# Graph attention and routed experts: slots between the third and fourth score step, three row scatters a turn for the next graph

## The chip, the core and the metric

The kernel runs on one core of a Trainium2 chip. The metric is the time of one execution in device microseconds (us); lower is better. A core has TensorE (PE: matrix products and transposes), VectorE (DVE), ScalarE (ACT), GpSimd (POOL) and SyncE (SP). Each has its own list of instructions and runs it in order; they wait for each other by semaphores.

## The reference

Sixteen graphs of 512 nodes with 128 features. With x normalised over its features (feat):

```python
h = feat @ W
logits = swap(h @ a_1) + h @ a_2 + (h @ a_12) @ swap(h)
e = where(adj > 0, leaky_relu(logits, 0.2), NEG_INF)
h_prime = softmax(e) @ feat
x = x + elu(feat @ W_1 + h_prime @ W_2)
```

Here a graph's attention runs over its own 512 nodes. Then the tokens, x normalised again, go through 16 experts of which the two with the highest gate logits count:

```python
topk_vals, topk_idx = top_k(xn @ gate_w + gate_b, 2)
moe = sum_k softmax(topk_vals)_k * (relu(xn @ w1[e_k] + b1[e_k]) @ w2[e_k] + b2[e_k])
x = x + layernorm(xn + moe) * gamma + beta
```

## The kernel before

The kernel has a **graph stage** and an **expert stage**. The graph stage ends with each token's normalised row written twice (once for each of its two experts) into a table in device memory, `expert_bins`, sorted by expert. The expert stage loads tiles of 128 rows of that table, runs the two products of their expert, and scatters the results.

A graph has 4 tiles (`TPG`) of 128 nodes. The graph stage is a software pipeline: `turns(body)` (line 258) runs `body(k)` on each engine with k from -2 to 18 (19 on GpSimd), and in a turn k each engine works on several graphs at once. `has(k, n)` says whether graph k - n exists. In turn k, in the order of the engines' lists:

- Graph k: scores (PE L733 and L734, DVE L923), with relu (ACT L563) and exponential (ACT L567). PE adds the mask `no_edge` to the product of queries and features; DVE joins it with the relu and finds the row minimum. There are four score steps a turn, one for each tile.
- Graph k - 1: transposes of the probabilities (PE L724), their copies (ACT L558 for tiles 0 to 2, DVE L931 for tile 3) and the products with the values (PE L742). ACT's copy of tile 2 waits for TensorE's product of tile 0 as well.
- Graph k - 2: ELU (DVE L937, L940, L948, L952; ACT L572), statistics of the rows (DVE L907, L912), one over the root of the variance on GpSimd (`rstds`, L475 and L480), normalised rows (DVE L969).
- Graph k - 3: row transposes (PE L773), gate logits (PE L781), the top two experts (DVE `gate`, L1043 to L1064), `ranks` (PE L752 and L754: how many tokens before this one go to the same expert), `slot` (DVE L1071 to L1089: the row number of each token in the table, from the ranks and a running count `base`). `slot` also needs `gate_exp` (ACT L615).
- Graph k - 4: eight row scatters (GpSimd L485, `scatter_row`), each an indirect DMA of 128 rows of 520 bytes, one for each tile and each of the two experts.
- Graph k + 1: feature transposes (PE L789, copied by ACT L590), queries, and at the turn's end the edge mask `no_edge` (DVE L901), made of the int32 adjacency of 128x2048 elements. The next turn's first score step waits for it.

**GpSimd's turn.** Its list in a turn is written by hand. Eight places for scatters stand between waits for steps of VectorE and ScalarE of graph k (`after_masked`: score step n done, `after_prob`: n exponentials done) and the two `rstds`. In a turn k before the change all eight places take rows of graph k - 4, whose slots were made in the turn before. The waits only place the scatters in time; the data do not need them.

**VectorE's turn** has, at its end: score steps 2 and 3, copy of tile 3, `slot(k - 3)`, `feature_shift`, `mask(k + 1)`, `rows(k - 2)`. **TensorE's** has scores 2, feature transposes of graph k + 1, ranks of graph k - 3, scores 3, values 1, queries, values 2 and 3. **ScalarE's** has, from the middle: exps 1, relu 2, features copy, rows_out, gate_exps, relu 3, exps 3, queries copy, exps 2, features.

**From stage to stage.** When the last `slot` is done, VectorE makes the table of tiles (L1112 to L1164), which TensorE helps to spread over the partitions (L838). SyncE and ScalarE write padding rows (L390, L659: eight DMAs each). SyncE waits for the table, the padding and all row scatters before it loads the first tile (L419).

Of the kernel before, what the change touches and what calls it, by code (L numbers as in the profile page):

```python
# [20 lines left out]
def graph_attention_and_routed_experts(nc, x, adj, W, a_1, a_2, a_12, W_1, W_2, gate_w, gate_b, w1, b1, w2, b2,  # L21
# [7 lines left out]
    K = 2  # L29
# [25 lines left out]
    with ExitStack() as ctx:  # L55
# [164 lines left out]
        def settle(eng):  # L220

            eng.sem_inc(s_settled[eng.engine.name], 1)
# [40 lines left out]
        def has(k, back):  # L263

            return not isinstance(k, int) or 0 <= k - back < G
# [178 lines left out]
        def _(pool):  # L444
# [47 lines left out]
            def after_prob(k, n):  # L492
                if has(k, 0):
                    pool.wait_ge(s_exp, k * TPG + n)

            def body(k, b, h):
                if has(k, 4):
                    pool.wait_ge(s_slot, k - 3)
                    pool.wait_ge(s_row_out, k - 3)
                    settle(pool)  # L500
                    scatter_row(k - 4, 0, 0)
                    after_masked(k, 0)
                    scatter_row(k - 4, 0, 1)
                    after_prob(k, 1)
                    scatter_row(k - 4, 1, 0)
                    after_masked(k, 1)
                    scatter_row(k - 4, 1, 1)
                if has(k, -2):
                    rstds(0, k + 3, s_mv1, s_rs1)
                if has(k, 4):  # L510
                    scatter_row(k - 4, 2, 0)
                if has(k, 2):
                    rstds(TPG, k - 1, s_mv2, s_rs2)
                if has(k, 4):
                    after_masked(k, 2)
                    scatter_row(k - 4, 2, 1)
                    after_masked(k, 3)
                    scatter_row(k - 4, 3, 0)
                    after_prob(k, 3)
                    scatter_row(k - 4, 3, 1)  # L520
            turns(body, 4)


# [176 lines left out]
        def _(pe):  # L700
# [96 lines left out]
            def body(k, b, h):  # L797
                if has(k, 1):
                    prob_transposes(k - 1, 0)
                if has(k, 0):  # L800
                    scores(k, b, 0)
                if has(k, 1):
                    prob_transposes(k - 1, 1)
                if has(k, 0):
                    scores(k, b, 1)
                if has(k, 3):
                    rows_transposes(k - 3)
                if has(k, 0):
                    features_products(k, b)
                if has(k, 3):  # L810
                    logits(k - 3)
                if has(k, 1):
                    prob_transposes(k - 1, 2)
                    prob_transposes(k - 1, 3)
                    values(k - 1, 1 - b, 0)
                if has(k, 0):
                    scores(k, b, 2)
                if has(k, -1):
                    features_transposes(k + 1)
                if has(k, 3):  # L820
                    ranks(k - 3)
                if has(k, 0):
                    scores(k, b, 3)
                if has(k, 1):
                    values(k - 1, 1 - b, 1)
                if has(k, -1):
                    queries(k + 1, 1 - b)
                if has(k, 1):
                    values(k - 1, 1 - b, 2)
                    values(k - 1, 1 - b, 3)  # L830
            turns(body)


# [57 lines left out]
        def _(dve):  # L891
# [106 lines left out]
            def body(k, b, h):  # L998
# [24 lines left out]
                    stats(k - 2, TPG, s_bn2, s_mv2)  # L1023
                if has(k, 0):
                    scores(k, 2)
                    scores(k, 3)
                if has(k, 1):
                    pt_copy(k - 1, 3)
                if has(k, 3):
                    slot(k - 3)  # L1030
                if has(k, -2):
                    feature_shift(k + 2)
                if has(k, -1):
# [248 lines left out]
```

## Time and profile before

| what | us |
|---|---|
| median of 3 runs | 612.57 |
| lowest and highest | 611.96, 614.91 |
| the profiled execution's own time | 614.96 |
| its span, first to last instruction | 613.2 |
| mean granted TensorE clock | 0.905 |

The graph stage takes the first 306 us, the hand-over to the expert stage up to about 330 us, the expert stage the rest. In the rows, a timeline line has the start, the busy time, the engine, the line of the kernel, the operation and what it writes and reads. In square brackets stands how long the engine was idle before it and what ended that. PEld are weight loads of TensorE. A granted clock of 1.00 is 2.4 GHz, 0.50 is 1.2 GHz.

### The profile page before, as it was taken

What the parts mean: (1) busy time and instruction counts of PE and PEld (TensorE: products, weight loads), DVE (VectorE), ACT (ScalarE), POOL (GpSimd) and SP (SyncE); (2) the same over time, 40 slices, a digit from 0 to 9 for tenths busy, and PEclk for the clock granted to TensorE, in tenths of its full rate; (3) what the DMA queues carried; (4) which work ended last, traced back from release to release, by engine and by line L of the source; (5) the groups of instructions that cost most, each with busy time, mean ns of one, the idle gap of its engine ahead of it and who ended that gap; (6) DMA issues with size and microseconds to landing.
All of it is one profiled execution on the core that took longest, in us unless ns stands there. A gap on an engine that the chain in (4) does not pass through costs nothing.

```text
span 613.2 us, 12119 instructions
## 1 busy us (share of the span) xinstructions
PE 464.1 (76%) x2950; PEld 372.8 (61%) x2972; DVE 388.1 (63%) x1669; ACT 309.5 (50%) x884; POOL 320.3 (52%) x354
## 2 busy tenths in 40 slices
PE   4799999999999898864205878787877877787862
PEld 3377776777777676663204767666766656676640
DVE  3338888888888776666457333355656566574675
ACT  2588777777777677532002534443444444344420
POOL 3001376776677675655750555555555554555550
PEclk9899999999999999985555877898898999888996
DMA  6138333433344433110135646636766766766622
GB/s 173 51 109 276 142 111 94 114 118 115 118 122 121 118 104 109 36 36 30 48 104 152 191 126 191 179 105 171 229 196 196 203 189 188 203 182 199 199 61 86
DMA packets 88836, 84.25 MB, mean 137 GB/s; under 512 B 11128, under 2 KB 75296, under 8 KB 88640
## 3 DMA queue, kind: packets, MB, share of 16 engines
q1 hardware_dynamic: 77216, 64.70, 37.2%
q0 software_dynamic: 8672, 16.93, 7.9%
q10 hardware_dynamic: 2880, 1.84, 1.0%
q8 instruction: 26, 0.43, 0.3%
q14 instruction: 42, 0.34, 0.2%
HBM read 61.19 MB, written 23.22 MB: 138 GB/s over the span
## 4 chain that ended last, share of the span: by engine, by line
PE 45%; DVE 20%; issue 11%; another core or an unknown queue 10%; ACT 9%; ACTq 2%; DMA 2%; DVEq 1%; SPq 0%; POOL 0%; POOLq 0%
PE bank L857 12%; PE bank L864 12%; PE bank L734 4%; ACT hidT L678 3%; PE bank L742 3%; PE bank L872 3%; DVE bn L907 3%; PE bank L764 3%; PE bank L724 2%; DVE prob L923 2%; PE bank L851 2%; DVE x_sb L952 2%; DVE no_edge L901 2%; DVE probT L931 1%
## 5 line engine op out<-in xcount | busy, mean ns | idle before, releaser
L526 POOL DMA_INDIRECT expert_results<-y,xg x143 | 140.6, 984 | 138.2 <-DVE y L1181 99.3
L678 ACT ACTIVATE hidT<-bank,b_cols 128x128 f32<-128x128 f32 x286 | 90.3, 368 | 138.0 <-PE bank L857 73.3
L485 POOL DMA_INDIRECT expert_bins<-row_out,slots x128 | 135.9, 1062 | 42.0 <-issue 31.3
L864 PE MATMUL bank<-w_sb,hidT 128*128 x572 | 104.2, 310 | 49.2 <-ACT hidT L678 42.9
L864 PEld LDWEIGHTS bank<-w_sb,hidT 128*128 128x128 f32 x572 | 85.7, 213 | 67.6 <-issue 66.7
L1178 DVE TENSOR_TENSOR bank<-bank,b_all 128x128 f32<-128x128 f32 x143 | 42.3, 296 | 105.8 <-PE bank L864 64.6
L857 PE MATMUL bank<-xgT,w_cur 128*128 128x128 f32 x572 | 98.0, 299 | 7.6 <-issue 6.0
L857 PEld LDWEIGHTS bank<-xgT,w_cur 128*128 128x128 f32 x572 | 85.3, 214 | 9.5 <-issue 7.5
L742 PEld LDWEIGHTS bank<-vh,probT 128*128 128x128 f32 x512 | 65.5, 195 | 28.0 <-issue 13.9
L742 PE MATMUL bank<-vh,probT 128*128 128x128 f32 x512 | 70.5, 282 | 11.0 <-DVE probT L931 8.4
L734 PE MATMUL bank<-featT,qT 128*128 128x512 f32 x128 | 67.1, 607 | 8.0 <-DVE no_edge L901 4.0
L923 DVE CUSTOM_DVE_ANT_0 prob<-bank,relu 128x512 f32<-128x512 f32 x64 | 43.8, 689 | 38.0 <-ACT relu L563 33.4
L1181 DVE SCALAR_TENSOR_TENSOR y<-bank,xg 128x128 f32<-128x128 f32 x143 | 50.2, 351 | 13.8
L475 POOL TENSOR_SCALAR var_eps<-mv 128x4 f32<-128x4 f32 x32 | 7.7, 242 | 90.9 <-DVE mv L912 90.6
L567 ACT ACTIVATE prob<-prob,row_min 128x512 f32<-128x512 f32 x64 | 45.7, 715 | 16.7 <-DVE row_min L923 16.7
L851 PE MATMUL bank<-ident,xg 128*128 128x128 f32 x143 | 42.4, 297 | 8.9 <-DMA xg<-expert_bins 6.9
L563 ACT ACTIVATE relu<-bank 128x512 f32<-128x512 f32 x64 | 38.0, 593 | 20.0 <-PE bank L734 19.5
L558 ACT COPY probT<-bank 128x512 f32<-128x512 f32 x48 | 28.1, 586 | 37.2 <-PE bank L742 22.9
L671 ACT COPY xgT<-bank 128x128 f32<-128x128 f32 x143 | 38.4, 269 | 11.2 <-issue 7.1
L872 PE MATMUL bank<-yy,ident 128*128 128x512 f32 x64 | 32.0, 625 | 7.1 <-DMA yy<-expert_results 7.1
L724 PEld LDWEIGHTS bank<-ident,prob 128*128 128x128 f32 x256 | 31.5, 149 | 9.6 <-issue 9.1
L724 PE MATMUL bank<-ident,prob 128*128 128x128 f32 x256 | 37.2, 279 | 0.1
(147 smaller groups left out, 717.4 us busy)
## 6 DMA issues: line engine op xcount, KB each, us to landing
w_cur<-in_L_ffn_w_dram SPq DMA_DIRECT2D x135, 128.0 KB
adj_sb<-in_adj_dram SPq DMA_DIRECT2D x16, 1024.0 KB
xg<-expert_bins SPq DMA_DIRECT2D x143, 65.0 KB
yy<-expert_results SPq DMA_DIRECT2D x16, 512.0 KB
x_sb<-in_x_dram SPq DMA_DIRECT2D x16, 256.0 KB
out_dram<-x_sb SPq DMA_DIRECT2D x16, 256.0 KB
expert_results<-y,xg POOLq DMA_INDIRECT x143
expert_bins<-row_out,slots POOLq DMA_INDIRECT x128
```

Source lines behind the costliest of these rows:

```text
L485: nc.gpsimd.indirect_dma_start(bins, bass.IndirectOffsetOnAxis(ap=slots[:, r, i, j:j + 1], axis=0), row_out[:, r, j, i, :], None).then_inc ...
L526: nc.gpsimd.indirect_dma_start(results[0:not_finished(t), :], bass.IndirectOffsetOnAxis(ap=xg[:, t % XS, D:D + 1].bitcast(U32), axis=0), y ...
L678: r = nc.scalar.activation(hidT[:, t % NB, c * P:(c + 1) * P], hidden_of(t, c), ACT.Relu, bias=b1_cols[:, bass.ds(e * FC + c, 1)])
L724: last = nc.tensor.transpose(bank[2 + i % 2][:, c * P:(c + 1) * P], prob[:, i, c * P:(c + 1) * P], ident[:, :])
L734: mm(bank[i % 2][:, :], qT[:, b, i * P:(i + 1) * P], featT[:, b, :], start=False, stop=True).then_inc(s_s, 1)
L742: last = mm(bank[6][:, i * P:(i + 1) * P], probT[:, i % 2, c * P:(c + 1) * P], vh[:, b, c, 0:D], start=(c == 0), stop=(c == TPG - 1))
L851: nc.tensor.transpose(xT_of(t), xg[:, t % XS, 0:D], ident[:, :]).then_inc(s_tx, 1)
L857: m1 = mm(hidden_of(t, c), w1_cur[:, t % WS, c * P:(c + 1) * P], xgT[:, t % NB, :], start=True, stop=True)
L864: m2 = mm(out_psum(t), hidT[:, t % NB, c * P:(c + 1) * P], w2_sb[:, bass.ds((e * FC + c) * D, D)], start=(c == 0), stop=(c == FC - 1))
L872: last = mm(sums_of(g).rearrange("p (a d) -> p a d", a=TPG), ident[:, :], yy[:, g % YB, :, j * D:(j + 1) * D], start=(j == 0), stop=(j == ...
L923: V.tensor_tensor_reduce(prob[:, i, :], bank[i % 2][:, :], relu4[:, i % 2, :], -ALPHA, 3e38, ALU.add, ALU.min, row_min[:, i:i + 1]).then_i ...
L1181: V.scalar_tensor_tensor(out=y[:, v, :], in0=out_psum(t), scalar=xg[:, v, D + 1:D + 2], in1=xg[:, v, 0:D], op0=ALU.mult, op1=ALU.add).then ...
```

## The change

On GpSimd, the eight places of turn k take rows 3 to 7 of graph k - 4 and then rows 0 to 2 of graph k - 3. The wait for a graph's slots and for the copy of its rows moves to the place of its row 0. On TensorE, `ranks(k - 3)` goes ahead of `features_transposes(k + 1)`. On VectorE, `slot(k - 3)` goes between score steps 2 and 3; it was behind the copy of tile 3.

```diff
@@ GpSimd @@
+            def scatter(g, n):
+                if has(g, 0):
+                    if n == 0:
+                        pool.wait_ge(s_slot, g + 1)
+                        pool.wait_ge(s_row_out, g + 1)
+                        settle(pool)
+                    scatter_row(g, n // K, n % K)
             def body(k, b, h):
-                if has(k, 4):
-                    pool.wait_ge(s_slot, k - 3)
-                    pool.wait_ge(s_row_out, k - 3)
-                    settle(pool)
-                    scatter_row(k - 4, 0, 0)
-                    after_masked(k, 0)
-                    scatter_row(k - 4, 0, 1)
-                    after_prob(k, 1)
-                    scatter_row(k - 4, 1, 0)
-                    after_masked(k, 1)
-                    scatter_row(k - 4, 1, 1)
+                scatter(k - 4, 3)
+                after_masked(k, 0)
+                scatter(k - 4, 4)
+                after_prob(k, 1)
+                scatter(k - 4, 5)
+                after_masked(k, 1)
+                scatter(k - 4, 6)
                 if has(k, -2):
                     rstds(0, k + 3, s_mv1, s_rs1)
-                if has(k, 4):
-                    scatter_row(k - 4, 2, 0)
+                scatter(k - 4, 7)
                 if has(k, 2):
                     rstds(TPG, k - 1, s_mv2, s_rs2)
-                if has(k, 4):
-                    after_masked(k, 2)
-                    scatter_row(k - 4, 2, 1)
-                    after_masked(k, 3)
-                    scatter_row(k - 4, 3, 0)
-                    after_prob(k, 3)
-                    scatter_row(k - 4, 3, 1)
+                after_masked(k, 2)
+                scatter(k - 3, 0)
+                after_masked(k, 3)
+                scatter(k - 3, 1)
+                after_prob(k, 3)
+                scatter(k - 3, 2)
@@ TensorE @@
                     scores(k, b, 2)
+                if has(k, 3):
+                    ranks(k - 3)
                 if has(k, -1):
                     features_transposes(k + 1)
-                if has(k, 3):
-                    ranks(k - 3)
@@ VectorE @@
                     scores(k, 2)
+                if has(k, 3):
+                    slot(k - 3)
+                if has(k, 0):
                     scores(k, 3)
                 if has(k, 1):
                     pt_copy(k - 1, 3)
-                if has(k, 3):
-                    slot(k - 3)
```

## Rows read from the trace of the kernel before

**Rows 1.** Page, part 1: busy us, share of the span, instructions, by engine.
```profile
PE 464.1 (76%) x2950; PEld 372.8 (61%) x2972; DVE 388.1 (63%) x1669; ACT 309.5 (50%) x884; POOL 320.3 (52%) x354
```
**Rows 2.** Stretches from mask end to mask end: length, busy times, clock, DMA share, GB/s.
```profile
151.71:168.12 16.41, 14.68 (x98) 11.39 (x100) 13.29 (x63) 11.92 (x28) 11.72 (x13) 1.00 0.37 114
168.12:183.87 15.75, 14.66 (x99) 11.35 (x100) 13.39 (x63) 11.91 (x28) 10.94 (x13) 1.00 0.41 119
...
233.06:250.11 17.05, 14.92 (x99) 11.42 (x100) 12.14 (x54) 11.07 (x25) 9.52 (x11) 1.00 0.34 98
```
**Rows 3.** Timeline of VectorE, end of the turn at 152 to 168.
```profile
163.54 0.69 DVE L923 CUSTOM_DVE_ANT_0 prob<-bank,relu 128x512 f32<-128x512 f32 x1
...
164.44 0.69 DVE L923 CUSTOM_DVE_ANT_0 prob<-bank,relu 128x512 f32<-128x512 f32 x1 [0.19 <-ACT relu L563]
...
165.05 0.69 DVE L931 COPY probT<-bank 128x512 f32<-128x512 f32 x1
...
165.66 0.21 DVE L1071 TENSOR_TENSOR place<-bank,base 128x64 f32<-128x64 f32 x1
...
166.62 0.28 DVE L1089 TENSOR_REDUCE slots<-picked 128x8 uint32<-128x128 f32 x1
...
166.90 1.22 DVE L901 TENSOR_SCALAR no_edge<-adj_sb 128x2048 bf16<-128x2048 int32 x1
```
**Rows 4.** Timeline of ScalarE and TensorE over the same turn's end.
```profile
165.17 0.72 ACT L567 ACTIVATE prob<-prob,row_min 128x512 f32<-128x512 f32 x1 [0.95 <-DVE row_min L923]
...
165.79 1.16 PE L742 MATMUL bank<-vh,probT 128*128 128x128 f32 x8 [0.60 <-DVE probT L931]
...
168.17 0.10 PEld L733 LDWEIGHTS bank<-no_edge,ident_bf 128*128 128x128 bf16 x1 [1.02 <-DVE no_edge L901]
...
169.46 0.60 ACT L563 ACTIVATE relu<-bank 128x512 f32<-128x512 f32 x1 [0.66 <-PE bank L734]
```
**Rows 5.** Timeline of GpSimd in two turns.
```profile
150.56 1.98 POOL L485 DMA_INDIRECT expert_bins<-row_out,slots  x1 [0.30 <-DVE slots L1089]
...
157.91 0.96 POOL L485 DMA_INDIRECT expert_bins<-row_out,slots  x1 [0.31 <-issue]
...
165.38 1.10 POOL L485 DMA_INDIRECT expert_bins<-row_out,slots  x1 [0.20 <-DVE row_min L923]
166.79 1.45 POOL L485 DMA_INDIRECT expert_bins<-row_out,slots  x1 [0.30 <-issue]
...
173.81 0.96 POOL L485 DMA_INDIRECT expert_bins<-row_out,slots  x1 [0.30 <-issue]
```
**Rows 6.** Timeline: ScalarE's third copy in three turns, the products and scatter before.
```profile
158.24 1.06 PE L742 MATMUL bank<-vh,probT 128*128 128x128 f32 x8
...
160.24 0.59 ACT L558 COPY probT<-bank 128x512 f32<-128x512 f32 x1 [2.45 <-PE bank L742]
...
176.00 0.59 ACT L558 COPY probT<-bank 128x512 f32<-128x512 f32 x1 [1.79 <-PE bank L742]
...
240.02 0.96 POOL L485 DMA_INDIRECT expert_bins<-row_out,slots  x1 [0.30 <-issue]
...
242.31 0.59 ACT L558 COPY probT<-bank 128x512 f32<-128x512 f32 x1 [3.16 <-remote]
```
**Rows 7.** Timeline of the stage's end and the hand-over.
```profile
280.13 2.08 PE L742 MATMUL bank<-vh,probT 128*128 128x128 f32 x8 [2.21 <-DVE probT L931]
...
305.53 0.28 DVE L1089 TENSOR_REDUCE slots<-picked 128x8 uint32<-128x128 f32 x1
...
307.46 1.08 POOL L485 DMA_INDIRECT expert_bins<-row_out,slots  x1 [0.31 <-issue]
...
315.86 0.81 DVE L1157 TENSOR_SCALAR diag<-ident,col 72x72 f32<-72x72 f32 x4 [0.55 <-DVE col L1151]
...
316.98 0.96 POOL L485 DMA_INDIRECT expert_bins<-row_out,slots  x1 [0.30 <-issue]
...
320.12 1.33 PE L838 MATMUL bank<-diag,ones 72*128 72x144 f32 x4 [18.27 <-remote]
```

## The prediction

> **What bounds the kernel now.** I read the page's busy line first [rows 1]: no engine is busy for more than 76% of the span, so the question is which waits close the loop of a turn of the graph stage. The table by stretches comes next, cut at the ends of successive writes of the edge mask (L901), which come once a turn [rows 2]. The full turns from the fifth on fall in groups: five of 15.74 to 15.77 us, three of 16.41 to 16.43 us, two of 17.04 and 17.05 us. TensorE's granted clock is at the higher level, 2.4 GHz (1.00), in all of them. Then the timeline of the end of one turn, engine by engine [rows 3 to 5]. On VectorE the third score step starts at 163.54, the fourth at 164.44 after 0.19 us of waiting for ScalarE, then the copy of the transposed probabilities at 165.05, the slot step from 165.66 to 166.90, and the mask from 166.90 to 168.12. TensorE waits 1.02 us for that mask. ScalarE waits 0.95 us for the fourth score step's result and then has 0.66 us of slack before the next turn's first relu.
>
> GpSimd does not look critical, but two pairs of rows say otherwise. First, its second scatter of a group takes 1.45 us when it starts 0.11 us before the mask (166.79 against 166.90), and 1.98 us when it starts 0.07 us after the mask's start (150.56 against 151.71 less 1.22); a free one takes 0.96 [rows 2, 3, 5]. Secondly, ScalarE's third copy of a turn, which opens the way to z_exp and with it to the rest of VectorE's turn, waits for TensorE's products. They end at 159.30 by the records (158.24 and 1.06), but the copy starts at 160.24. In the three turns shown it starts 2.33, 2.19 and 2.29 us after the start of GpSimd's last scatter of a row (157.91 to 160.24, 173.81 to 176.00, 240.02 to 242.31) [rows 5, 6]. The last of these is a turn in which a row has eight scatters and not seven, because no first rstd step stands between: it takes 17.05 us. I read this so: while GpSimd issues scatters back to back, the signals of the other engines come late, and they come about 1 us after the last scatter of the row has ended. So a scatter that is held up lengthens the turn, though GpSimd has idle time later.
>
> **The change, part by part.** The profiled execution took 614.96 us, with a span of 613.2. The median of the runs shown is 612.57, and I carry differences over to the median.
>
> (a) Slot step before the fourth score step, on VectorE. Nothing is added. The step takes 1.24 us up to the end of its last instruction [rows 3], and 1.16 of issue, since neighbours overlap by some 0.08. It stands now after the third score step (0.69 us after its start), so the fourth starts 0.69 + 1.16 = 1.85 us after the third and not 0.90: 0.95 later. What it waits for is there by then: gate_exp is before the relu of the fourth score step in ScalarE's order, and VectorE waits for that relu until 164.44 already now; the ranks are before the fourth score product in TensorE's. The 0.19 us wait for the relu is covered now, so the mask comes 0.20 us earlier relative to the third score step (+3.16 and not +3.36).
>
> (b) Who waits for the later fourth score step. TensorE: its fourth value product waits for the copy at 165.05, which now ends near 166.70; behind it stand eight products (165.79 to 166.95) and four transposes whose issue I estimate at half of the eight's less the overlap, so that TensorE is ready some 1.42 us after the copy's end, at 168.12. It starts now at 168.17 [rows 4]: no loss, and no gain from the earlier mask either. ScalarE: its exps(3) to features chain moves by 0.95 and has 0.66 + 0.09 (instructions back to back overlap) = 0.75 of slack: the first relu is 0.20 us late. Summed from sc0 to sc0, ScalarE's and VectorE's loop becomes 15.85 us, 0.10 over the short turns. Its cover is thin: any further delay here counts in full.
>
> (c) Ranks before the feature transposes, on TensorE. The same instructions. Feature transposes come some 0.4 us later and delay the fourth score product by that; its relu stands behind ScalarE's featT copy, row copy and gate_exp, which hide it: 0, between 0 and +0.4 a turn. In this trace the signals after the many tiny rank products are the ones that come late, and the feature transposes' signal now stands behind them; that is rival C.
>
> (d) Three scatters moved one turn forward, on GpSimd. Each turn still issues eight and calls settle once. The first scatter of a graph must wait for slots that the same turn makes. They are ready 0.69 + 1.24 = 1.93 us after the third score step's start; GpSimd starts this place now at +1.84 (165.38), and will start it near +2.13. With 1.10 us and the 0.30 between scatters the next one starts at +3.53, in the middle of the mask (+3.16 to +4.38). That is the case of the 1.98 us scatter [rows 5]: every turn becomes one with a held-up scatter, where so far three of ten were. The delay goes to the row's last scatter, as in the turn at 150 to 160: 6.20 us after the mask's end (157.91 against 151.71), and the ScalarE copy 8.53 after it. From that copy (160.24) to the third score step (163.54) pass 3.30, and to the mask's end 4.38. New turn: 8.53 + 3.30 + 4.38 = 16.21 us. Bounds: 15.69 if the signals do not hang on GpSimd (15.75 less the 0.06 us of (b)), 16.41 as the three slow turns.
>
> The row fits a rule of the Trainium skill (SBUF — State Buffer, "Who interferes with whom"): VectorE and GpSimd share a port pair that one holds for a whole instruction, and descriptor writing of a GpSimd DMA is locked out by VectorE operations in a two-port mode. By that page alone the moved scatter would cost idle GpSimd time and nothing more, and the sum would be near zero. The late signals of [rows 6] aren't in it.
>
> (e) The end of the stage. The last graph's slots are ready at 305.81; GpSimd is still busy with the graph before and starts their eight scatters at 307.46, the last at 316.98, ended 317.94 [rows 7]. After the change its queue is empty by then, and they start about 0.2 us after the slots: 1.45 us earlier. TensorE's spread of the table starts at 320.12 though VectorE had made its input by 316.67 (315.86 and 0.81); I put that to the same late signals, so it follows the last scatter: -1.45. In the turn after the last scores the slot step now stands ahead of the copy for which the fourth value product waits (280.13) [rows 7], so products and row transposes behind them are up to 1.1 us late. The ranks' late signal there hides most of it: +0.4. Later slots push the scatters before by 0.3. Together -0.7, between -1.5 and +1.5.
>
> **Sum.** Five short turns: 5 x 0.46 = +2.3. The first turn with scatters (15.55 now, no held-up scatter): +0.66. The three slow turns: 3 x -0.20 = -0.6. The turn of 17.04: between -0.8 and +0.5, taken as -0.4. The last two full turns, eight scatters in a row: +0.4 each. Steady part +2.8; end -0.7; together +2.1 us: 617.1 against the profiled 614.96, and **614.7** against the median.
>
> **The rivals.**
> A. The signals are late for a reason of their own. Then turns stay at 15.69 to 15.85 us (0 to +1.2 in all) and only the end gains 1.45: 612.3, between 610.5 and 613.5. For it: the copy at 160.24 is also where a slow turn starts on other engines. Against it: the eight-scatter turn.
> B. Faster. The last ranks and slots are freed from the queue of scatters: if GpSimd is idle when the last table is begun, TensorE's 3.4 us between VectorE's diagonals (316.7) and 320.12 goes for the most part, and turns are no longer than before: -3.4 - 0.7 = 608.5. It decides if the late signals end with the amount of queued scatters and not with the last one. Against it: eight scatters still lie beside the table.
> C. Slower by a new wait. The feature transposes' signal comes behind the ranks', ScalarE's featT copy waits for it, and gate_exp, which the slot step now needs before the fourth score step, stands behind that copy in ScalarE's order; VectorE then waits in the middle of its turn. A turn so hit would take the 17.05 us of the longest now [rows 2], 0.84 over the new turn; in five of twelve turns this is +4.2: 618.9. It decides from a signal that is 0.6 us later than now, since the copy starts that long after it.
> That the change doesn't do what it says (scatters only wait for slots and end where they did) is within A, at 613.
>
> **How the numbers follow.** Forecast 0.42 (612.5 to 617), A 0.25, B 0.16, C 0.17. A measurement of this kernel can tell about 0.5%, 3.06 us, from no change: 609.51 to 615.63. Faster: most of B and a little of A, 0.19. Slower: nearly all of C and the upper third of the forecast, 0.31. Same: 0.50. The range reaches from B's centre to C's near side: 608.5 to 618.5.
>
> **What would show it.** Right: in the new trace the second scatter after each second rstd step starts inside the mask and takes about 2 us; mask-to-mask stretches are all near 16.2; the fourth score step starts 1.85 us after the third; the last eight scatters start within 0.3 us of the last slots. Wrong: short turns stay at 15.75 beside held-up scatters (A); TensorE's table spread starts within 1 us of the diagonals (B); VectorE's slot step shows idle time before it, waiting for gate_exp (C).

## The result and the profile after

The changed kernel took 637.5 us (median of 634.83, 637.5 and 640.89) against 612.57: a ratio of 1.041, 95% interval 1.035 to 1.047. The forecast was 614.7, with a range up to 618.5. The profiled execution took 634.83 us, 19.9 more than that of before; the difference is smaller than that of the medians, 24.9, because the profile after is of the fastest of its executions and the one before (614.96) of one slower than all three listed. First the busy line of the page after, which answers to [rows 1]:

```profile
PE 469.6 (74%) x2950; PEld 374.6 (59%) x2972; DVE 386.6 (61%) x1669; ACT 309.7 (49%) x884; POOL 319.1 (50%) x354
```

TensorE is busy for 5.5 us more than before, PEld for 1.8, and no other engine for more, so most of the new time is idle time. The stretches from mask end to mask end (length, busy times of the five engines, TensorE's granted clock, DMA share, GB/s) answer to [rows 2]:

```profile
57.05:72.80 15.75, 14.47 (x101) 11.40 (x101) 13.21 (x63) 11.80 (x28) 2.53 (x4) 1.00 0.42 152
72.80:91.61 18.81, 15.32 (x102) 11.38 (x101) 13.16 (x63) 11.80 (x28) 12.81 (x13) 1.00 0.30 99
165.57:184.04 18.47, 15.87 (x101) 12.23 (x102) 13.27 (x63) 12.01 (x28) 11.11 (x13) 0.91 0.36 101
184.04:202.59 18.55, 14.78 (x102) 11.40 (x102) 13.29 (x64) 11.80 (x28) 11.13 (x13) 1.00 0.34 101
```

The first stretch has no scatters yet (GpSimd busy for 2.53 us) and takes 15.75 us. The next one has them and takes 18.81. From there every turn takes 18.37 to 18.55 us, in place of 15.55 to 17.05. A granted clock of 0.91 beside one of 1.00 makes no difference to the length (18.47 and 18.55). Eleven turns add 25.9 us; the hand-over gives back 1.1 (19.7 us from the last slots to the first load of the expert stage before, 18.6 after). The expert stage, which the change doesn't touch, took 282.5 us and not 287.7; I have no explanation for these 5.2 us and don't count them for the change; in the traces of experiments 1 to 4, on one chip, the unchanged expert stage takes 274.5 to 285.5 us. With 0.3 more before the first of these turns and 0.1 less between the last mask and the last slots this is the difference of the spans, 19.9.

Where in the turn? VectorE around the mask at 164.35, answering to [rows 3], and its next gate step (start, busy, engine, line, operation; in brackets the idle time before it and what ended it; `remote` stands where the profile finds no instruction that ended close before the signal):

```profile
161.29 0.69 DVE L926 CUSTOM_DVE_ANT_0 prob<-bank,relu 128x512 f32<-128x512 f32 x1
...
162.88 0.28 DVE L1093 TENSOR_REDUCE slots<-picked 128x8 uint32<-128x128 f32 x1
163.07 0.68 DVE L926 CUSTOM_DVE_ANT_0 prob<-bank,relu 128x512 f32<-128x512 f32 x1
...
164.35 1.22 DVE L904 TENSOR_SCALAR no_edge<-adj_sb 128x2048 bf16<-128x2048 int32 x1
...
171.60 0.38 DVE L915 BATCH_NORM_AGGREGATE mv<-bn 128x2 f32<-128x6 f32 x4
174.64 0.23 DVE L1047 TENSOR_TENSOR logit<-bank,gate_bias 128x64 f32<-128x64 f32 x1 [2.66 <-remote]
```

The order around the slots runs as meant, without a gap. The new time is the 2.66 us before the gate step, which adds a bias to the gate logits that TensorE made. TensorE's product of these logits, its next wait, ScalarE's third copy and GpSimd's scatters in the same turn:

```profile
170.78 0.96 PE L784 MATMUL bank<-gate_sb,x2T 128*128 128x16 f32 x8
...
176.95 0.18 PE L757 MATMUL bank<-member,before_bf 128*128 128x16 bf16 x1 [2.33 <-DVE member L1068]
```
```profile
175.53 0.59 ACT L561 COPY probT<-bank 128x512 f32<-128x512 f32 x1 [3.48 <-remote]
```
```profile
163.97 1.72 POOL L485 DMA_INDIRECT expert_bins<-row_out,slots  x1 [1.04 <-DVE row_min L926]
165.99 0.96 POOL L485 DMA_INDIRECT expert_bins<-row_out,slots  x1 [0.30 <-issue]
...
172.31 0.96 POOL L485 DMA_INDIRECT expert_bins<-row_out,slots  x1 [0.30 <-issue]
```

The product ended at 171.74 and VectorE takes it in at 174.64, 2.9 us later; TensorE, which needs VectorE's member in turn, waits 2.33 us at 176.95. VectorE's 174.64 is 2.33 us after the start of the row's last scatter (172.31), the same distance as that of the late third copy before the change (2.19 to 2.33, [rows 5, 6]). TensorE itself isn't late: by the trace's semaphore records its next signals, for work that ended at 172.66, were noted at 174.68 and 174.74, one after the other behind that of the logits (174.62). Before the change the gate step mostly stood on the other side of that lateness. Two turns of before, the ordinary one from 168.12 and the one of 17.04 us from 199.61:

```profile
174.22 0.23 DVE L1043 TENSOR_TENSOR logit<-bank,gate_bias 128x64 f32<-128x64 f32 x1
...
207.24 0.23 DVE L1043 TENSOR_TENSOR logit<-bank,gate_bias 128x64 f32<-128x64 f32 x1 [1.62 <-remote]
```
```profile
172.94 0.96 PE L781 MATMUL bank<-gate_sb,x2T 128*128 128x16 f32 x8
...
204.42 0.96 PE L781 MATMUL bank<-gate_sb,x2T 128*128 128x16 f32 x8
```

The logits product ended 5.78 and 5.77 us after the mask's end (172.94 + 0.96 - 168.12; 204.42 + 0.96 - 199.61). Once VectorE took it in 0.32 us later (it waited 0.09), and once 1.86 us later, 1.95 us after the last scatter's start. So the kernel before stood on an edge and fell off it in one of its eleven turns; the changed kernel falls off it in every turn but the first with scatters, in which it is the third copy that waits. For the same product the changed kernel has 6.17 us after the mask's end in this turn (170.78 + 0.96 - 165.57), 5.99 in six of the eleven.

The stage's end after, answering to [rows 7], engine by engine (SPq is SyncE's queue of DMA issues):

```profile
331.69 0.28 DVE L1093 TENSOR_REDUCE slots<-picked 128x8 uint32<-128x128 f32 x1
...
340.58 0.75 DVE L1161 TENSOR_SCALAR diag<-ident,col 72x72 f32<-72x72 f32 x4
```
```profile
335.63 1.07 POOL L485 DMA_INDIRECT expert_bins<-row_out,slots  x1 [0.30 <-issue]
...
345.23 0.96 POOL L485 DMA_INDIRECT expert_bins<-row_out,slots  x1 [0.31 <-issue]
```
```profile
341.38 1.33 PE L841 MATMUL bank<-diag,ones 72*128 72x144 f32 x4 [10.71 <-issue]
```
```profile
333.81 14.13 SPq L390 DMA_DIRECT2D expert_bins<-pad_rows  x8
350.57 1.43 SPq L419 DMA_DIRECT2D xg<-expert_bins  x3
```

The last graph's scatters start 3.66 us after its slots and not 0.2, because GpSimd still issues those of the graph before. The table's spread starts at 341.38, as soon as the diagonals are ready and 4.8 us before the last scatter has ended. What the first load at 350.57 comes behind is SyncE's eight pad writes, which end at 347.94.

### The profile page after: what moved, and what is told of

Same layout as the page of the kernel before. It is cut to its first block, busy times and chain, and to the rows that moved or that the text cites. A ratio compares the mean times of both kernels' runs of the same rounds, so it can differ in the third digit from the quotient of the medians.

```text
span 633.1 us, 12142 instructions
## 1 busy us (share of the span) xinstructions
PE 469.6 (74%) x2950; PEld 374.6 (59%) x2972; DVE 386.6 (61%) x1669; ACT 309.7 (49%) x884; POOL 319.1 (50%) x354
## 4 chain that ended last, share of the span: by engine, by line
PE 30%; DVE 24%; issue 23%; another core or an unknown queue 9%; ACT 6%; DMA 3%; SPq 3%; ACTq 1%; DVEq 1%; POOL 0%; POOLq 0%
PE bank L860 10%; PE bank L867 10%; DVE prob L926 3%; DVE bn L910 3%; PE bank L854 2%; ACT hidT L681 2%; PE bank L875 2%; PE bank L737 2%; DVE no_edge L904 2%; DVE row_out L972 1%; DVE z L943 1%; DVE x_sb L955 1%; DVE mv L915 1%; DMA xg<-expert_bins 1%
## 5 line engine op out<-in xcount | busy, mean ns | idle before, releaser
L867 PE MATMUL bank<-w_sb,hidT 128*128 x572 | 101.4, 304 | 41.5 <-ACT hidT L681 35.7
L867 PEld LDWEIGHTS bank<-w_sb,hidT 128*128 128x128 f32 x572 | 83.3, 207 | 59.2 <-issue 58.2
L745 PEld LDWEIGHTS bank<-vh,probT 128*128 128x128 f32 x512 | 68.9, 204 | 34.0 <-issue 17.2
L745 PE MATMUL bank<-vh,probT 128*128 128x128 f32 x512 | 72.1, 289 | 14.9 <-DVE probT L934 13.5
L737 PE MATMUL bank<-featT,qT 128*128 128x512 f32 x128 | 71.7, 644 | 2.4 <-ACT qT L599 0.9
L926 DVE CUSTOM_DVE_ANT_0 prob<-bank,relu 128x512 f32<-128x512 f32 x64 | 43.9, 687 | 41.1 <-ACT relu L566 25.9
```

The source lines that it names most:

```text
L737: mm(bank[i % 2][:, :], qT[:, b, i * P:(i + 1) * P], featT[:, b, :], start=False, stop=True).then_inc(s_s, 1)
L745: last = mm(bank[6][:, i * P:(i + 1) * P], probT[:, i % 2, c * P:(c + 1) * P], vh[:, b, c, 0:D], start=(c == 0), stop=(c == TPG - 1))
L867: m2 = mm(out_psum(t), hidT[:, t % NB, c * P:(c + 1) * P], w2_sb[:, bass.ds((e * FC + c) * D, D)], start=(c == 0), stop=(c == FC - 1))
L926: V.tensor_tensor_reduce(prob[:, i, :], bank[i % 2][:, :], relu4[:, i % 2, :], -ALPHA, 3e38, ALU.add, ALU.min, row_min[:, i:i + 1]).then_i ...
```

## The experiments

**S** is the theory that the lateness follows GpSimd's row of scatters: signals due during the row arrive about 2 us after the start of its last scatter. **V**, the rival, says that the new order on VectorE and TensorE costs the time by itself, wherever the scatters stand. The experiments ran on four chips, with the kernel before timed on the same chip; on these four it took 604.4, 537.3, 537.0 and 603.3 us. This turned out to be a result of its own. The kernel before was traced only once, on the chip of the first result, and the changed kernel there and on the third of the four; where turns of different chips are compared below, that is said. Times of a scatter, a gate step or a copy below are from the end of the turn's mask unless a row says otherwise.

**1. GpSimd's part alone** (chip with 604.4 us). The changed kernel less its two moves on TensorE and VectorE (lines with a minus are those of the changed kernel):

```diff
-                if has(k, 3):
-                    ranks(k - 3)
                 if has(k, -1):
                     features_transposes(k + 1)
+                if has(k, 3):
+                    ranks(k - 3)
...
-                if has(k, 3):
-                    slot(k - 3)
-                if has(k, 0):
                     scores(k, 3)
...
+                if has(k, 3):
+                    slot(k - 3)
```

> Only GpSimd's part of the change: rows 0 to 2 of the next graph in the last three places, slot step and ranks where they were. Theory S (signals of the other engines come late while GpSimd issues a row of scatters, and the row now ends later against the gate logits): the first scatter waits for slots made at the turn's end, so the row ends even later than in the changed kernel, turns of 18.5 us or more, time 637 us or more. Rival V (the lengthening comes from VectorE's and ScalarE's loop, by the slot step ahead of the fourth score step): nothing of that is in here, so turns near 15.8 to 16.4 us and 611 to 616 us.

Measured: 628.2 us, 1.037 (1.033 to 1.041). One turn (mask end 129.52), GpSimd's last scatter of the row, ScalarE's third copy:

```profile
129.52:147.34 17.82, 15.15 (x100) 11.37 (x100) 13.41 (x63) 11.94 (x28) 10.78 (x13) 1.00 0.32 104
```
```profile
137.12 0.96 POOL L485 DMA_INDIRECT expert_bins<-row_out,slots  x1 [0.31 <-issue]
```
```profile
139.46 0.59 ACT L561 COPY probT<-bank 128x512 f32<-128x512 f32 x1 [3.86 <-remote]
```

Nine turns between the first and the last with scatters take 17.80 to 17.91 us, bar one of 18.41. Most of the cost is there without any move on the other engines (3.7% here, 4.1% on the first chip): V falls as the only cause. The row ends late (last scatter at 7.60) and the copy comes 2.34 us after that scatter's start. The size expected by S, 18.5 us a turn and 637 us or more, was missed. Nor is it the changed kernel's path: the gate step waits only 0.1 to 0.9 us here in eight of these nine turns, and the third copy (idle 3.86 us in the line above) carries the cost.

**2. The order alone** (same chip). The slots ahead of the fourth score step and the ranks ahead of the feature transposes, GpSimd as before:

```diff
+                if has(k, 3):
+                    ranks(k - 3)
                 if has(k, -1):
                     features_transposes(k + 1)
-                if has(k, 3):
-                    ranks(k - 3)
...
+                if has(k, 3):
+                    slot(k - 3)
                 if has(k, 0):
                     scores(k, 3)
...
-                if has(k, 3):
-                    slot(k - 3)
```

> Only the orders of VectorE and TensorE: slot step between score steps 3 and 4, ranks before the feature transposes; GpSimd's list as before the change. Theory S: GpSimd's row of seven keeps its pauses and its place, VectorE waits for the gate logits no longer than before, turns 15.85 to 16.4 us, 612 to 618 us. Rival V: turns of about 18.5 us and 635 us or more.

Measured: 607.7 us, 1.005 (1.002 to 1.009). One turn (mask end 119.86), then VectorE's third and fourth score steps and mask, GpSimd, and ScalarE's third copy:

```profile
119.86:136.03 16.17, 14.76 (x103) 11.33 (x101) 13.30 (x64) 11.80 (x28) 11.42 (x13) 1.00 0.33 114
```
```profile
115.58 0.69 DVE L923 CUSTOM_DVE_ANT_0 prob<-bank,relu 128x512 f32<-128x512 f32 x1
...
117.37 0.68 DVE L923 CUSTOM_DVE_ANT_0 prob<-bank,relu 128x512 f32<-128x512 f32 x1
...
118.64 1.22 DVE L901 TENSOR_SCALAR no_edge<-adj_sb 128x2048 bf16<-128x2048 int32 x1
```
```profile
118.83 1.87 POOL L485 DMA_INDIRECT expert_bins<-row_out,slots  x1 [0.31 <-issue]
...
126.06 0.96 POOL L485 DMA_INDIRECT expert_bins<-row_out,slots  x1 [0.30 <-issue]
```
```profile
128.30 0.58 ACT L558 COPY probT<-bank 128x512 f32<-128x512 f32 x1 [2.13 <-PE bank L742]
```

This is the turn that the prediction described: a second scatter held up beside the mask (1.87 us), the row's last at 6.20, the copy at 8.44, the turn 16.17. Of the nine turns between the first and the last with scatters eight take 16.03 to 16.17 us and one 16.82.

**3. The changed kernel with a shorter row** (same chip). The last scatter of the row moved behind the first square-root step:

```diff
-                scatter(k - 4, 6)
                 if has(k, -2):
                     rstds(0, k + 3, s_mv1, s_rs1)
+                scatter(k - 4, 6)
                 scatter(k - 4, 7)
```

> The changed kernel, but the scatter that stands last in the row (row 6 of graph k - 4) goes behind the first rstd step, so that the row before the gate logits' signal has six scatters and not seven, and ends 1.27 us earlier. Theory S: VectorE's wait of 2.65 us before the gate step becomes 1.3 us or vanishes, turns 16 to 17.2 us, 616 to 625 us. Rival V: turns stay at 18.5 us, 634 to 641 us.

Measured: 613.0 us, 1.015 (1.011 to 1.019); nine turns of 16.89 to 17.00 us between the first with scatters (17.34) and the last (18.21). One (mask end 123.48), GpSimd's last scatter of the row, VectorE's gate step:

```profile
123.48:140.47 16.99, 14.74 (x103) 11.31 (x101) 13.27 (x63) 11.92 (x28) 11.12 (x13) 1.00 0.38 109
```
```profile
128.96 0.96 POOL L485 DMA_INDIRECT expert_bins<-row_out,slots  x1 [0.30 <-DVE row_min L926]
```
```profile
131.07 0.23 DVE L1047 TENSOR_TENSOR logit<-bank,gate_bias 128x64 f32<-128x64 f32 x1 [1.16 <-remote]
```

Against the first trace of the changed kernel, on another chip, the row ends 1.26 us earlier and the turn is 1.5 us shorter. The gate step still waits, and comes 2.11 us after the last scatter's start.

**4. The kernel before with a longer row** (same chip). One scatter moved ahead of the first square-root step:

```diff
+                if has(k, 4):
+                    scatter_row(k - 4, 2, 0)
                 if has(k, -2):
                     rstds(0, k + 3, s_mv1, s_rs1)
-                if has(k, 4):
-                    scatter_row(k - 4, 2, 0)
```

> The kernel before the change, but the first rstd step goes behind the fifth scatter of the turn, so that the row has eight scatters and not seven; nothing else. Theory S: every turn becomes like the one of 17.05 us that had eight scatters in a row, +1.3 us in each of nine turns, 622 to 628 us. Rival V, and any theory in which GpSimd's scatters do not delay others: GpSimd is idle later in the turn and the first rstd step is needed only at its end, so 611 to 615 us.

Measured: 614.7 us, 1.017 (1.014 to 1.021), 10.3 us over the kernel before at the median. The trace is of an execution of 622.28 us; its eleven turns with scatters take 16.89 to 17.11 us each, together 9.4 us more than those of before in the first trace. One (mask end 124.02), GpSimd, ScalarE:

```profile
124.02:141.05 17.03, 14.99 (x100) 11.37 (x100) 13.37 (x64) 11.92 (x28) 10.91 (x13) 1.00 0.37 108
```
```profile
130.97 0.96 POOL L485 DMA_INDIRECT expert_bins<-row_out,slots  x1 [0.30 <-issue]
```
```profile
133.18 0.58 ACT L558 COPY probT<-bank 128x512 f32<-128x512 f32 x1 [3.08 <-PE bank L742]
```

No scatter was added, and the turn is 1.3 us longer than an ordinary one of before: the copy is again 2.21 us behind the last scatter's start. In this kernel the end of the row sets the turn.

**5 to 8. Four more rows, on a chip where nothing depends on them** (537.3 us). The kernel before with a row of six, and of five (there the scatter before it is moved too); the change with the ranks back behind the feature transposes; and the change with two places for the next graph (each place takes the scatter one earlier). The edits of the first and the last:

```diff
-                    scatter_row(k - 4, 1, 1)
                 if has(k, -2):
                     rstds(0, k + 3, s_mv1, s_rs1)
                 if has(k, 4):
+                    scatter_row(k - 4, 1, 1)
                     scatter_row(k - 4, 2, 0)
```
```diff
-                scatter(k - 3, 0)
+                scatter(k - 4, 7)
                 after_masked(k, 3)
-                scatter(k - 3, 1)
+                scatter(k - 3, 0)
                 after_prob(k, 3)
-                scatter(k - 3, 2)
+                scatter(k - 3, 1)
```

> The kernel before the change, with the last scatter of the row (expert 1 of tile 1) moved behind the first rstd step: a row of six scatters, then two. Theory S (ScalarE's third copy starts some 2.2 us after the start of the row's last scatter, unless TensorE is later): the row ends 1.27 us earlier, the copy is then set by TensorE, 0.2 us earlier in the short turns and 0.8 in the three slow ones; turns of 15.5 to 15.7 us, 2 to 4 us less than before in all. Rival F (the row's length doesn't matter below seven, VectorE and ScalarE set the turn): within 1 us of before.

> The kernel before the change, with a row of five scatters ahead of the first rstd step and three behind it. Theory S: nothing more to gain than with six, since TensorE's products end where they do; 2 to 4 us less than before, unless the three scatters behind the rstd step (about 12 us after the mask) delay the second rstd step and the rows. Rival F: within 1 us of before.

> The changed kernel with TensorE's feature transposes ahead of the ranks again. Theory S: what is late is the gate logits' signal, far ahead of both; TensorE gains up to 0.5 us a turn at most, turns of 18.0 to 18.5 us, 4% over before to within 1%. Rival C of the prediction (the feature transposes' signal comes late behind the ranks): turns fall to 16.2 to 17 us.

> The change with two places in a turn instead of three for the next graph: place 6 takes the last row of graph k - 4, so the first scatter after the second rstd step waits for no slots; all else as in the changed kernel. Theory S: GpSimd starts its group again 1.8 us after the third score step, two scatters lie ahead of the mask's end, and the row ends 6.2 us after it, as in the run with the orders of VectorE and TensorE alone: turns of 16.17 us, and time within 3 us of that run's. Rival V: turns stay at 18.5 us, since slot step, ranks and fourth score step stand as in the changed kernel.

Measured: 538.0 (1.002, 0.999 to 1.004), 538.6 (1.002, 1.000 to 1.005), 538.4 (1.000, 0.998 to 1.002) and 537.8 us (1.001, 0.998 to 1.004). In the last two, which were traced on a chip with late signals too (experiment 10), the scatters behind the mask start at the same times there to a few hundredths, yet no gate step waits for a late signal, and the turns are 15.55 to 15.92 us but for a first one of 16.03 and the last. What S expected of these four runs didn't come. They showed that the lateness isn't there on every chip.

**9. The changed kernel once more** (a third chip, 537.0 us), with three of the variants:

> The changed kernel as it is, once more, beside the kernel before and the three others on one chip. The last batch ran on a chip on which the kernel before takes 537.3 us, and there no engine started late while GpSimd issued its row of scatters; the two earlier ones (612.6 and 604.4 us) had such late starts. If this chip has them: turns of 18.4 to 18.5 us with VectorE idle for 2.6 us ahead of the gate step, ratio 1.035 to 1.045. If it has none: turns of 15.7 us, ratio 0.998 to 1.003. A theory that the change costs something by its order alone (the slots ahead of the fourth score step, the ranks ahead of the feature transposes) expects a cost of over 0.5% on either kind of chip.

Measured: 537.3 us, 1.002 (1.000 to 1.005). Two turns; then, in the turn from 151.01, VectorE, TensorE, GpSimd and ScalarE:

```profile
151.01:166.72 15.71, 14.47 (x101) 11.40 (x101) 13.16 (x64) 11.80 (x28) 11.66 (x13) 1.00 0.40 119
166.72:182.64 15.92, 14.63 (x102) 11.33 (x101) 13.29 (x64) 11.80 (x28) 11.15 (x13) 1.00 0.38 117
```
```profile
157.35 0.19 DVE L1047 TENSOR_TENSOR logit<-bank,gate_bias 128x64 f32<-128x64 f32 x1
```
```profile
156.04 0.96 PE L784 MATMUL bank<-gate_sb,x2T 128*128 128x16 f32 x8
```
```profile
149.41 1.72 POOL L485 DMA_INDIRECT expert_bins<-row_out,slots  x1 [1.04 <-DVE row_min L926]
...
157.76 0.96 POOL L485 DMA_INDIRECT expert_bins<-row_out,slots  x1 [0.30 <-DVE mv L915]
```
```profile
158.91 0.59 ACT L561 COPY probT<-bank 128x512 f32<-128x512 f32 x1 [1.59 <-PE bank L745]
```

This is the same kernel as in the first trace, with the same scatters: the first takes 1.72 us, the last starts 6.75 us after the mask's end (6.74 there). But the gate step starts 0.35 us after the product's end, before the row's last scatter has started, and the turn takes 15.71 us where it took 18.47. The two differ by 2.76 us a turn, and nearly all that the change costs hangs on the lateness: here it costs 0.2% (nothing to 0.5%).

> The kernel before with the seventh scatter of the row moved behind the first square-root step, so the row that follows the mask ends 1.27 us earlier. Late-signal theory, on a chip that has them: the third copy comes at the mask's end + 7.9 instead of + 8.2 and the turns of 16.4 and 17.0 us go, turns of 15.6 us throughout, 2 to 4 us faster than before (0.993 to 0.997). On a chip without: 1.000 to 1.003, as on the last one (1.0017). The rival (the number of scatters in a turn counts, not where they stand) expects no gain on either.

> The change with two places for the next graph's rows instead of three: the scatters run at -2.45, -0.97 and 1.14 to 6.19 us from the mask's end (last run's trace), as in the run with the order alone. If only the end of the row counts, on a chip with late signals: third copy at + 8.4, turns of 16.2 us, ratio 1.004 to 1.009. If the rest of the change (less the third place) costs by itself, turns above 16.8 us, ratio above 1.015. On a chip without late signals 1.000 to 1.003 in either case.

> The change with the ranks put back behind the feature transposes. On a chip with late signals: if what VectorE waits 2.65 us for at the gate step is the gate logits' signal as such, held back until the row has ended (+ 6.74, + 2.3), the turn stays at 18.4 to 18.5 us and the ratio at 1.035 to 1.045; if it needs the ranks product ahead of the logits, the gate step starts at + 6.3 without a wait and the turn follows the third copy (+ 9.0 to 9.3), 16.9 to 17.1 us, ratio 1.015 to 1.02. On a chip without: 1.000 to 1.003, as last time.

Measured, on the same chip: 536.3 (1.000, 0.996 to 1.003), 537.5 (0.999, 0.996 to 1.002) and 537.6 us (1.001, 0.997 to 1.004); the same picture.

**10. The three open ones on a chip that has late signals** (603.3 us). The ranks put back:

> The change with the ranks behind the feature transposes, sent again in the hope of a chip on which signals come late. There: if VectorE's wait at the gate step is the logits' signal as such, held back until the row has ended, turns of 18.4 to 18.5 us; if it needs the ranks product ahead of the logits, the gate step at + 6.3 without a wait and turns of 16.9 to 17.1 us behind the third copy. On a chip without late signals: turns of 15.7 us, 0.998 to 1.003.

Measured: 630.4 us, 1.044 (1.035 to 1.054). Two turns; VectorE's gate step, and GpSimd's last scatter of the row, in the first:

```profile
164.47:182.81 18.34, 14.70 (x103) 11.34 (x101) 13.28 (x63) 11.90 (x28) 11.14 (x13) 1.00 0.35 102
182.81:201.14 18.33, 16.37 (x103) 12.45 (x101) 13.29 (x64) 11.91 (x28) 11.14 (x13) 0.91 0.34 102
```
```profile
173.40 0.23 DVE L1047 TENSOR_TENSOR logit<-bank,gate_bias 128x64 f32<-128x64 f32 x1 [2.52 <-remote]
```
```profile
171.22 0.96 POOL L485 DMA_INDIRECT expert_bins<-row_out,slots  x1 [0.30 <-issue]
```

With the order of ranks and feature transposes put back the wait is still there, 2.5 us of it, so that order isn't its cause. Two places in place of three:

> The change with two places for the next graph's rows. On a chip with late signals: turns of 16.2 us if only the end of the row counts (third copy at + 8.4), above 16.8 us if the rest of the change costs by itself. On a chip without: turns of 15.7 us, 0.998 to 1.003.

Measured: 605.9 us, 1.007 (1.003 to 1.012). One turn (mask end 154.06), and from the turn from 121.87 GpSimd's last scatter of the row and ScalarE's third copy:

```profile
154.06:170.23 16.17, 14.75 (x103) 11.32 (x101) 13.32 (x63) 11.79 (x28) 11.37 (x13) 1.00 0.34 116
```
```profile
128.06 0.96 POOL L485 DMA_INDIRECT expert_bins<-row_out,slots  x1 [0.30 <-issue]
```
```profile
130.30 0.59 ACT L561 COPY probT<-bank 128x512 f32<-128x512 f32 x1 [2.13 <-PE bank L745]
```

So it is the third place that turns a cost of 0.7% into one of 4% (the run above, on this chip, has it and differs otherwise only in the ranks): with it the scatters behind the mask start at 0.42 and end with one at 6.74, with two places they start at 1.14 and end with one at 6.19. The kernel before with a row of six:

> The kernel before with the row one scatter shorter. On a chip with late signals, late-signal theory: turns of 15.6 us throughout, 0.993 to 0.997; the rival (the number of scatters in a turn counts): no gain. On a chip without: 0.997 to 1.003.

Measured: 602.8 us, 0.997 (0.993 to 1.002). Its turns are 15.55 to 15.61 us up to the last full one (17.56), with none of the 16.4 and 17.0 us, as S expects; the last one and the time itself, which can't be told from no change, are not as S expected (15.6 throughout, 0.993 to 0.997). No version here is measurably faster than the kernel before.

## Why the prediction was wrong

**Direction and size.** Forecast was +2.1 us; measured +24.9 at the median. "Slower by over 0.5%" had a chance of 0.31, and all of it was thought to come from rival C or the forecast's upper end. The reason that the prediction gave, signals that come late until the row of scatters is over, was right; what it did with it was too narrow.

**(a) and (b), the order, held.** The fourth score step starts 1.78 us after the third (163.07 less 161.29; forecast 1.85) and the mask 3.06 after it (forecast 3.16). On the chips without late signals the turns of the changed kernel are 15.70 to 15.73 us, bar two of 15.91 and 15.92 and the last, and those of the kernel before with a row of six 15.55 to 15.61: 0.17 a turn on the mean of ten (experiment 9's chip), where (b) said 0.10.

**(c), the ranks, held.** With the ranks back (630.4 us) the cost is all there; the turns, on another chip, are 0.1 to 0.2 us shorter.

**(d) is the step that failed**, in two ways. First its size: it let the first scatter start 0.2 us after the slots, in time for the second to be the one that is held by the mask. GpSimd had nothing queued then, and the scatter started at 163.97, 0.81 us after the slots' end (162.88 + 0.28). So the first scatter was the one beside the mask, and the row's last came at 6.74 in place of 6.20 (5.69 before). By (d)'s own sum the copy and the turn would follow by 0.54, to 16.75 us. Two smaller terms of the prediction don't add up either: the lower bound of 15.69 takes 0.06 off for (b), which had added 0.10, and the sum has twelve turns with scatters where eleven end with a mask (0.4). The rule of the Trainium skill that was weighed there (SBUF — State Buffer, "Who interferes with whom") and this trace agree that GpSimd's DMA issue is held by VectorE: the scatter beside the mask takes 1.72 us and ends 0.12 us after it, on the chips with and without late signals alike. In which mode the mask runs no run shows.

Secondly, and this is most of it: (d) followed one late signal, that of the third copy, and not the others due in the same row. I had not looked at the gate logits' signal 2 us before it, because VectorE didn't wait for it in the turns that I read. It is the first signal in the row's later part. The order on VectorE shifts its product by 0.21 us against the mask (5.78 to 5.99, experiments 2, 3 and 10), and with the third place the scatters behind the mask start at 0.42, 1.69, 2.96, 4.22, 5.48 and 6.74, where before they started at 0.43, 1.69, 3.13, 4.42 and 5.69. The gate step then comes at 9.07 in place of 5.9 to 6.2, and what follows it on VectorE up to the mask can't be made up: the 2.66 us of waiting are the 2.72 us of the turn (15.75 to 18.47) but for 0.06. The turn of 17.04 us, which the prediction took as an oddity worth -0.4, was this case in the trace of before: VectorE waited 1.62 us for the same signal.

**(e), the end of the stage.** Forecast -0.7, measured -1.1, but not by the forecast's way: the last scatters start 3.66 us after the slots, and the spread of the table doesn't wait for them. In the trace of before VectorE's signal for the spread was noted 3.41 us after the diagonals' end, at 320.08, 3.1 us after the last scatter's start, as (e) supposed; after the change it isn't late, though scatters are still being issued. Why not is open.

**The rivals.** A (signals late for a reason of their own) falls where signals are late: experiments 1, 3 and 4 move the lateness by moving scatters. On the chip without late signals a turn takes 15.71 us, near A's 15.69 to 15.85. B's sign, the spread within 1 us of the diagonals, is there, and its gain isn't: SyncE's pad writes stand in the spread's place. C (the slot step waits for gate_exp) doesn't occur: VectorE isn't idle before the slot step in any turn up to the last mask. Its kind, a wait on VectorE that takes up a late signal, was right, at a step that it didn't name.

**What stays open.** The row's end sets when most held signals come. Between the first and the last turn with scatters, in eight kernels, the first step that waits over a microsecond for a held signal starts 1.9 to 2.4 us after the start of the row's last scatter, bar one at 1.4 in experiment 1 (a second step can be later, as the third copy at 175.53 in the first trace after, 3.22 us). S is too simple in two places. Early in a row nothing is late: in all traces the first late signal of TensorE in a turn is of work that ended 5.78 us or more after the mask's end, though the row has run since the mask. And in experiments 1, 2 and 10 (two places) the logits' signal is often let through about 0.5 us after the start of a scatter, in experiment 1 while the row still runs. What decides whether it is held is only bracketed, by the product's end and the start of the fifth scatter behind the mask. 5.78 and 5.69: held for over a microsecond in one turn of seven before, in none of ten in experiment 4. 5.78 and 6.34 (experiment 1): VectorE waits 0.1 to 0.9 us, and 2.0 once, with the product at 6.76. 5.99 and 6.20 (experiments 2 and 10): 0 to 0.35 us, 1.0 once. 5.99 and 5.48 (the changed kernel, experiment 3, and 10 with the ranks back): held in every one. The later product and the earlier fifth scatter weren't taken apart.

Two rivals for the cause of the lateness weren't tested. One is that the scatters' transfers hold the signals, and not GpSimd's issuing: a kernel in which GpSimd computes for as long, in place of issuing scatters, wasn't tried. The other is the recording of the trace. The nine traces with late signals hold 5,898 to 6,699 records of semaphore updates, the eight without 12,613 to 12,723, for kernels that make nearly the same number: where signals are late, half of the records are missing. Both may have one cause, or the recording may be part of the lateness; every execution listed here comes with a recorded span and clock, so no run tells how these kernels go without recording. Why some chips hold signals and others don't is open too.

## What to carry to other kernels

When a trace shows one signal arriving late beside a long row of scatters, list every signal that falls due in that row, those nobody waits for today included, and price each as if it were held until about 2 us after the last scatter's start. An outlier among equal turns (one of 17.04 in eleven) is the cheapest place to see the next failure. And time such an order on more than one chip, and without recording if that can be done: the same two kernels stood 4.1% apart on one and within 0.5% on another.

## What the runs showed of the hardware

Beside a row of scatters issued 1.27 us apart, signals of TensorE reach VectorE and ScalarE late in three of the five batches of runs (before at 612.6, 604.4 and 603.3 us), that of the logits by 2.9 to 3.1 us in the changed kernel's steady turns, and without delay in the other two (537.3 and 537.0); the last four batches were on four different chips. In the first 70 us, where no scatter has been issued yet, no signal of TensorE is over 0.2 us late in any of the seventeen traces. The scatters themselves take the same time on both kinds, 0.96 us free and 1.72 beside the mask. SyncE is slower as well: its eight pad writes beside the scatters of the hand-over, in the changed kernel on a chip without late signals:

```profile
293.64 4.04 SPq L390 DMA_DIRECT2D expert_bins<-pad_rows  x8
```

That is 4.04 us against 14.13 in the first trace after. The expert stage, which has scatters throughout, takes 229 us there (308.64 to the end at 537.6) and 274 to 288 on the others. The same lateness is in it: of the 325 to 344 signals of TensorE that each trace of the slower chips records there, 165 to 182 were noted over 0.2 us after the work had ended; the other traces record 417 to 429 each, and none of these is late. How much of the 50 us and more hangs on it wasn't tested.

On an idle GpSimd a scatter starts 0.81 us after what it waits for is ready (163.16 to 163.97), where one with nothing to wait for follows 0.30 us after the one before.
